# The band matrices of two depthwise filters, stored by step and by pieces of four channels

## The reference, cut to what matters

```python
def _dwconv(x, w):                 # x: (batch, time, channel), w: (channel, taps)
    K = w.shape[1]
    xt = jnp.pad(jnp.transpose(x, (0, 2, 1)), ((0, 0), (0, 0), (K - 1, 0)))
    y = jax.lax.conv_general_dilated(xt, w[:, None, :], (1,), 'VALID', ..., feature_group_count=w.shape[0])
    return jnp.transpose(y, (0, 2, 1))
...
paths = jnp.stack([_dwconv(v, fir_s)..., _dwconv(v, fir_m)..., _dwconv(v, fir_l)..., delta_path, v...], axis=3)
```

## Time and profile before

| | us |
|---|---|
| median of 3 runs | 965.83 (963.97 to 968.57) |
| the profiled execution: its own time | 969.41 |
| the profiled execution: its span | 967.6 |
| TensorE busy | 719.3 (74% of the span) |
| VectorE busy | 681.5 (70%) |
| ScalarE busy | 531.1 (55%) |
| DMA engines, queue q1 | 17.6% of the span |

### The profile page before, as it was taken

How to read it: one execution, slowest core, us unless ns; L and a number is a source line. 1 busy time by engine, 2 the same in 40 slices (tenths; PEclk the granted TensorE clock), 3 DMA queues, 4 the chain that set the end, 5 groups by cost and what they waited for, 6 DMA issues and landing times. The chain is left out here.

```text
span 967.6 us, 16500 instructions
## 1 busy us (share of the span) xinstructions
PE 719.3 (74%) x6146; PEld 419.8 (43%) x6146; DVE 681.5 (70%) x958; ACT 531.1 (55%) x978; POOL 284.4 (29%) x238
## 2 busy tenths in 40 slices
PE   3850008886766547786598697999998989999995
PEld 1320004432545547775354254444444844445542
DVE  4999985967844798446679782799999734545442
ACT  5888854653423433555445345999999214443332
POOL 0000000000201000000033400699999156566661
PEclk9985557988899758899788899999999699999998
DMA  5640000000894000100300002920000911111100
GB/s 203 217 143 0 0 0 23 1 0 0 223 245 97 4 2 3 25 3 3 111 1 1 11 22 78 393 83 0 1 0 1 337 42 46 39 43 36 45 26 6
DMA packets 35473, 60.78 MB, mean 63 GB/s; under 512 B 7771, under 2 KB 22107, under 8 KB 35010
## 3 DMA queue, kind: packets, MB, share of 16 engines
q1 hardware_dynamic: 32514, 53.42, 17.6%
q0 software_dynamic: 2880, 6.30, 2.2%
HBM read 54.46 MB, written 6.82 MB: 63 GB/s over the span
## 5 line engine op out<-in xcount | busy, mean ns | idle before, releaser
L2041 ACT ACTIVATE xT<-x_tr,moe_b 128x64 f32<-128x64 f32 x320 | 67.6, 360 | 115.5 <-PE x_tr L2008 115.5
L1982 PE MATMUL x_hid<-w,moe_xt 128*64 x160 | 74.6, 610 | 0.8 <-DVE moe_xt L2139 0.6
L1985 PE MATMUL x_hid<-h,moe_xt 128*64 128x512 f32 x160 | 74.6, 610 | 0.0
L1996 PE MATMUL x_y<-w,xT 128*64 x320 | 73.3, 382 | 1.8 <-ACT xT L2041 1.8
L1999 PE MATMUL x_y<-hs,xT 128*64 128x256 f32 x320 | 73.3, 382 | 0.0
L1756 DVE TENSOR_TENSOR_SCAN w<-r_bank,w 128x512 f32<-128x512 f32 x56 | 69.6, 1246 | 3.2 <-POOL w L1716 3.2
L1170 POOL TENSOR_TENSOR path<-path,mix_pr 128x1280 f32<-128x1280 f32 x12 | 28.7, 2421 | 132.9 <-DVE mix_pr L1405 132.9
L224 PE MATMUL bad_sum<-spike_bad,ones 128*128 128x16 f32 x2 | 0.6, 384 | 83.9 <-ACT spike_outside L190 83.9
L1624 PE MATMUL r_bank<-recur_h_other,w1h 128*128 128x512 f32 x128 | 60.2, 592 | 0.2 <-ACT recur_h_other L1665 0.2
L1618 PE MATMUL r_bank<-hs,eye 128*128 128x512 f32 x112 | 57.2, 592 | 1.2 <-PEq L1099 1.2
L1716 POOL TENSOR_TENSOR w<-w,recur_h_other 128x512 f32<-128x512 f32 x32 | 37.7, 1180 | 65.6 <-ACT recur_h_other L1665 59.6
(11 more groups left out here) (297 smaller groups left out, 2006.4 us busy)
## 6 DMA issues: line engine op xcount, KB each, us to landing
spike_wbuf<-in_gW SPq DMA_DIRECT2D x8, 1280.0 KB, 6.4
w<-in_w1T SPq DMA_DIRECT2D x8, 1024.0 KB, 12.1
w<-in_w2T SPq DMA_DIRECT2D x8, 1024.0 KB, 9.0
fir_band<-in_band_l SPq DMA_DIRECT2D x11, 512.0 KB
fir_band<-in_band_m SPq DMA_DIRECT2D x11, 312.0 KB
mix_st<-in_band_l SPq DMA_DIRECT2D x5, 512.0 KB
xT<-in_xT SPq DMA_DIRECT2D x4, 512.0 KB, 6.4
xT<-in_xT SPq DMA_DIRECT2D x2, 1024.0 KB, 6.2
```

The lines of the kernel that those rows point to most:

```text
L1982: nc.tensor.matmul(hid_bank[n][side(0), :], xt[:, c, side(0)], m.w1[:, bass.ds(e, 1), c, cols].rearrange("p o n -> p (o n)"), start=(c == ...
L1985: last = nc.tensor.matmul(hid_bank[n][side(1), :], xt[:, c, side(1)], w1_copy[:, g % 2, c, cols], start=(c == 0), stop=(c == C - 1), skip_ ...
L1996: nc.tensor.matmul(y_bank[side(0), :], ht[:, k, side(0)], w2[:, bass.ds(e, 1), k, :].rearrange("p o n -> p (o n)"), start=(k == 0), stop=( ...
L2041: nc.scalar.activation(ht[:, k, side(x)], turned[:, side(x)], ACT.Relu, bias=b1[:, bass.ds(e[x], 1), k]).then_inc(s.ht_ready, 1)
```

## The change

The band matrices are laid out in another order by the host, which is not part of the measured time: first the step of 16 channels, then the piece of 4 channels in it, then the input time (128 or 78 rows), then 4 channels x 64 outputs. A step of `band_l` is then one contiguous region of 512 KB, of `band_m` one of 312 KB. The piece of one partition is 4 x 64 x 4 bytes = 1 KB, and rows of one piece follow each other at a distance of 1 KB. What arrives on the chip, and where, is the same as before. The transfers, their number, their sizes, their waits and all compute instructions are the same; a transfer reads four pieces of 1 KB for each partition instead of one of 4 KB.

```diff
+FIR_STEP = N // P * 4
+FIR_PIECE = 4
...
-    STEP = PER * G
+    STEP = FIR_STEP
...
-                now = slice(s * STEP, (s + 1) * STEP)
-                sp.dma_start(band[i][:, 0], d.band_l[:, now, :]).then_inc(band_in[i], 16)
-                sp.dma_start(band[i][BAND_M:, 1], d.band_m[:, now, :]).then_inc(band_in[i], 16)
+                for f, first, x in ((0, 0, d.band_l), (1, BAND_M, d.band_m)):
+                    to = band[i][first:, f].rearrange("p (k c) i -> p k (c i)", c=FIR_PIECE)
+                    sp.dma_start(to, x[s].rearrange("k p n -> p k n")).then_inc(band_in[i], 16)
...
+def by_piece(band):
+
+    pieces = band.reshape(band.shape[0], -1, FIR_STEP // FIR_PIECE, FIR_PIECE * CH)
+    return pieces.transpose(1, 2, 0, 3)
...
-    lay["band_m"] = bands(lay.pop("fir_m"))[BAND_M:]
-    lay["band_l"] = bands(lay.pop("fir_l"))
+    lay["band_m"] = by_piece(bands(lay.pop("fir_m"))[BAND_M:])
+    lay["band_l"] = by_piece(bands(lay.pop("fir_l")))
```

## The result

The changed kernel takes 968.96 us (median of 16 runs) against 965.6 us for the kernel before (16 runs). The ratio is 1.0034, with a 95% interval of 1.002 to 1.0048: it is slower, by 3.4 us. 12.5 us less had been forecast. The profiled execution has a span of 971.0 us, against 967.6.

The account below looks back on a forecast made before the run. The prediction took one stage's band loads, at a full DMA share but low rate, as the bound. Gain 12.4 + 0.8 - 0.7 = 12.5 us, so 965.8 - 12.5 = 953.3 us; range 948.5 to 960.

Parts of the forecast that it names:

- What bounds the stage: Between the barriers at 240 and 309.9 us, loads set the pace: DMA share 0.91 to 0.99, only 219 to 261 GB/s.
- 13 engines for `band_m`, 14 packets on the busiest: Band loads before the change: 13 engines carry 8 + 6 packets of 4 KB a step, the other three 8.
- 262 ns for each packet: Band loads before the change: 3.67 us a step over 14 packets of 4 KB on the busiest engines.
- The same size at another distance: 4 KB rows: w1T's, 4 KB apart, take 159 ns; the bands', 64 KB apart, 262; distance taken as the visible difference.
- Part 1: Band loads in the new layout: 56 pieces at 47.1 ns, 2.64 us a step instead of 3.67; twelve steps gain 12.4 us.
- Part 2: First refill, the load of step 3: lands 5.03 us after issue instead of 5.82, 0.8 us earlier.
- Part 3: Issuing the 33 transfers on SyncE: no cost expected, though more pieces may bring single issues of up to 1,807 ns.
- Part 4: TensorE's lower clock, 3.1 us a step, no longer hidden for two or three steps: 0.7 us lost, from 0 to 1.5.
- (d): Rival, 7%: slower; loads limited on the receiving side, and smaller packets add 0.41 us a step, 971 us.
- The rule that the prediction names beside (d): Band packets: about 3 fixed cycles each, so 1 KB pieces cost 7% more; 3.92 us a step, kernel some 3 us slower.
- (c): Rival, 5%: no change; this stage's loads are slow per byte for a receiving-side reason, layout does not matter, 966 us.

## Why the prediction was wrong

**What bounds the stage** was read rightly: the loads, at a full DMA share and a low rate, and what is lost in the stage is lost in the kernel.

**13 engines for `band_m`, 14 packets on the busiest** stood (as many small packets after as before), but "262 ns for each packet" was a mean over unlike packets. Of those in the table above, 32% take at most 170 ns and the others up to twice that and more. I divided the step by 14 and asked why a packet takes 262 ns, where the question was which packets do.

**"The same size at another distance" is the step that failed.** I compared w1T (4 KB distance, 159 ns) with the bands (64 KB, 262 ns) and took the distance as the cause, "the difference that I can see". There was another in the code: w1T and w2T are written to 128 partitions, `band_m` to 78, 64 of which are the upper half. The runs put this in its place: distance alone 1.0009, place alone 216 to 234 against 335 to 341 GB/s. And the trace of before refutes the distance by itself. I used the mean of 245 to 250 us, 251 GB/s, against a cause on the receiving side; it speaks against TensorE's reading only, since `band_m` was being written there as well. Two stretches of half a microsecond, before TensorE reads any band:

```profile
244.00:244.50 0.50, 0.50 (x5) 0.42 (x4) 0.50 (x2) 0.41 (x1) 0.00 (x0) 1.00 1.06 434
245.00:245.50 0.50, 0.50 (x5) 0.26 (x4) 0.50 (x2) 0.41 (x2) 0.00 (x0) 1.00 1.14 246
```

In the first, all 51 packets take 159 to 164 ns, with rows 64 KB apart; in the second, none of 30 is under 180, and the median is 305. Between the two the first `band_l` ends: its 16 completion notes come from 244.28 to 244.94 us, and the 13 of the first `band_m` from 245.31 to 246.61. Nor did the figures of the Trainium skill that the prediction sets beside the distance ("DMA: Bandwidth & Descriptors", "Latency and other measured facts") support it: the half rate is theirs at 4 MB and more, and at their smallest distance, 512 KB, they have 207 of 214 GB/s.

**Part 1** (2.64 us a step) rested on it. 47.1 ns a piece was right where all 128 rows are loaded: 3.0 us for 64 pieces. With 78 rows neither size comes near the full rate: 3.62 us a step with 4 KB rows by step, 4.04 with 1 KB.

**Part 2** (0.8 us earlier) came out 0.6 us later: 6.42 us from issue to use, 6.03 with 4 KB rows by step, and 5.48 against 4.73 with 128 rows in 1 KB and 4 KB. Here, too, the missing rows cost and so do the small packets. **Part 3** held: issues of 0.37 and 0.48 us, one of 1.48 behind two whole steps in the queue, none of them waited for. **Part 4:** the clock did fall, more than before (0.58, 0.50 and 0.55 in the three stretches from 260 to 275 us, against 0.58, 0.74 and 1.00), and the waits had stayed. What it cost was not measured apart; the loads' own later end, 3.5 us, leaves little for it.

**The rival (d)** had the kind of the outcome, with 7%: 971 with 0.41 us a step, measured 969 and 0.24. The loss is smaller than the 0.5% under which I had said that nothing can be told; with 16 runs each its interval is 0.20 to 0.48%. 0.24 is what the 32 pieces of `band_l` alone would cost at 7.4 ns. That `band_m`, held by its place, does not pay for its smaller packets fits the number, but no run shows it, and 0.24 is about as large as what chance makes between two profiled executions. The rule that the prediction names beside (d) from the Trainium skill ("DMA: Bandwidth & Descriptors", "Why small descriptors are slow (HBM only)"), 7% and some 3 us, came nearest. That shows nothing for it: at full rate the runs have 3.0 us a step for 1 KB against 2.5 for 4 KB, nearly 20%. (c) and (d) named "a reason on the receiving side" but no row that could have raised their chance. The rate in half microseconds at the start of the stage, above, would have. Later in the stage it swings as well, between 112 and 371 GB/s from 262 to 300 us, but so does `band_l` alone.

**Open:** how rows are dealt out to engines when there are 78, 80, 96 or 104 of them; the order of their times is not explained by a count. So for 78 rows it is shown that the partial load is what is slow, not how much of it is the place and how much the 13 engines. And with `band_l` on all partitions and 64 rows of `band_m` on the upper half, a step took 3.60 us, where sharing alone asks for 16 x 159 ns = 2.54: together they lose more than sharing explains, and no run shows why.

## What to carry to other kernels

When a DMA stream is slow at a full share, split its mean by transfer first: look at the rate in slices shorter than one transfer where the order of the transfers is known, best at the start of the stage, and ask which transfer has another shape than the fast ones elsewhere in the kernel. A swing alone does not tell: a single kind of load with gaps between its starts swings too. A load to part of the partitions can cost more than the rows it saves; filling it up to all 128 with zeros loaded 24% more bytes in the stage and made this kernel about 0.8% faster. Rows of 4 KB beat rows of 1 KB (159 ns for 4 KB against 4 x 47 = 188), and collecting rows that lie 64 KB apart gained nothing.

## What the runs showed of the hardware that I had not expected

- 64 rows to partitions 64 to 127 go at 202 to 227 GB/s at a full share, and beside a second transfer on all partitions at 216 to 234 in two stretches; to partitions 32 to 95, in the same mix and stretches, at 335 to 341.
- The same in single packets of 4 KB: median 159 ns with 64 rows to partitions 32 to 95 beside a full transfer, 279 ns with 64 rows to partitions 64 to 127.
- A transfer of 96 rows on 16 engines (3.76 us a step with `band_l`) is slower than one of 128 rows (2.88), and one of 104 rows slower still (4.07).
